# Opening of a four-layer graph kernel: x loaded whole, normalization and transposes two groups ahead

## What is computed

```python
h = relu(layernorm(x))
Wh = h @ W
e = leaky_relu(Wh @ a_src + (Wh @ a_dst).T)      # 0.2 below zero
h_attn = softmax(where(adj > 0, e, -9e15)) @ Wh
# dense branches from Wh: fe1/fe2, bcdt/abp, hz/out -> h_enh, hs
g = sigmoid(silu(ln([h_attn, hs] @ g1 + g1_b)) @ g2 + g2_b)
x = x + ln(g * h_attn + (1 - g) * hs + h_enh)
```

## Time and profile before

| what | us |
|---|---|
| three runs, median (lowest to highest) | 2624.14 (2617.22 to 2624.57) |
| profiled execution, its time | 2621.8 |
| its span, first to last instruction | 2620.1 |
| opening (first arithmetic of layer 0 starts) | 129.13 |
| mean granted TensorE clock | 0.95 |

### The profile page before, as it was taken

One profiled execution on the slowest core, in us unless ns is written; L12 is line 12 of the kernel. 1 busy time (PEld: TensorE's weight loads), 2 busy tenths in 40 slices (PEclk: granted clock), 3 DMA queues, 4 the chain that ended last, 5 costly groups with the idle time before them and its releaser, 6 DMA issues. The chain is left out here.

```text
span 2620.1 us, 45995 instructions
## 1 busy us (share of the span) xinstructions
PE 2309.3 (88%) x17238; PEld 1726.9 (66%) x17238; DVE 1836.5 (70%) x2939; ACT 1403.2 (54%) x2238; POOL 113.0 (4%) x124
## 2 busy tenths in 40 slices
PE   3489989889898896599995799999889999999998
PEld 2367767667676664488883577777635666666667
DVE  3396686777868764211115889898869889988896
ACT  3455545556454553466655545454436555655565
POOL 1000000100000000000000000000000000000000
PEclk8789999999999998799997899999989999999999
DMA  8343314224111100322221111112121111111110
GB/s 194 43 82 57 61 45 65 53 61 69 35 36 45 43 23 33 97 88 76 80 68 40 46 61 62 66 60 68 40 83 35 49 33 45 49 49 33 41 33 25
DMA packets 64523, 149.01 MB, mean 57 GB/s; under 512 B 10224, under 2 KB 15856, under 8 KB 63344
## 3 DMA queue, kind: packets, MB, share of 16 engines
q1 hardware_dynamic: 54560, 108.19, 13.3%
q0 software_dynamic: 5760, 33.56, 7.7%
q10 hardware_dynamic: 4048, 5.18, 0.6%
HBM read 172.05 MB, written 41.94 MB: 82 GB/s over the span
## 5 line engine op out<-in xcount | busy, mean ns | idle before, releaser
L1834 PE MATMUL bank<-VB,ph 128*128 128x257 f16 x2048 | 523.5, 281 | 97.0 <-DVE VB L1778 34.6
L1835 PE MATMUL bank<-VB,ph 128*128 128x257 f16 x2048 | 522.2, 280 | 0.0
L195 PE MATMUL bank<-s_row,kT_hi 128*128 128x512 f16 x1024 | 306.4, 381 | 6.8 <-DMA s_row<-qT_d 4.9
L1834 PEld LDWEIGHTS bank<-VB,ph 128*128 128x128 f16 x2048 | 204.1, 100 | 142.6 <-DVE pl L1773 55.8
L1353 PE MATMUL bank<-VA,ph 128*128 128x257 f16 x1024 | 281.9, 275 | 16.4 <-DVE pl L1025 10.9
L1838 PE MATMUL bank<-VB,pl 128*128 128x257 f16 x1024 | 292.0, 285 | 0.0
L2440 PE MATMUL bank<-VA,ph 128*128 128x257 f16 x1024 | 280.5, 274 | 3.0 <-ACT w_later_hi L2301 2.4
L1354 PE MATMUL bank<-VA,ph 128*128 128x257 f16 x1024 | 281.7, 275 | 0.0
L1355 PE MATMUL bank<-VA,pl 128*128 128x257 f16 x1024 | 281.6, 275 | 0.0
L2442 PE MATMUL bank<-VA,pl 128*128 128x257 f16 x1024 | 280.0, 273 | 0.0
L2441 PE MATMUL bank<-VA,ph 128*128 128x257 f16 x1024 | 280.0, 273 | 0.0
(11 more groups left out here) (322 smaller groups left out, 4760.9 us busy)
## 6 DMA issues: line engine op xcount, KB each, us to landing
mask<-mask_d SPq DMA_DIRECT2D x256, 256.0 KB, 2.8
mask_d<-in_adj POOLq DMA_DIRECT2D x8, 2048.0 KB, 23.4
xg<-in_x SPq DMA_DIRECT2D x16, 512.0 KB, 4.6
xg<-x SPq DMA_DIRECT2D x16, 512.0 KB, 4.2
x<-xo POOLq DMA_DIRECT2D x16, 512.0 KB, 2.9
w_d<-wr SPq DMA_DIRECT2D x8, 512.0 KB, 2.6
f<-w_d SPq DMA_DIRECT2D x8, 512.0 KB, 8.0
x<-xg SPq DMA_DIRECT2D x8, 512.0 KB, 3.9
```

The lines of the kernel that those rows point to most:

```text
L195: last = nc.tensor.matmul(out_ap, st, mv, start=(i == 0), stop=(i == len(todo) - 1))
L1834: nc.tensor.matmul(acc, p_hi, v_at(V, 0, t), start=first, stop=False)
L1835: last = nc.tensor.matmul(acc, p_hi, v_at(V, 1, t), start=False, stop=final and not weighted)
```

## The change

x is loaded whole, in five transfers on SP, ahead of the dense weights (moved from ACT's queue to SP's, fe1 first). wc moves to ACT's queue. Every statistic has a place of its own, so waits on reuse go. PE makes hT(1) ahead of Wh(0) and hT(g+2) behind Wh(g); ACT makes hT_hi(g+1), h(g+2), then keeps Wh(g); DVE takes moments three groups ahead. The bias rows lie as 18 partitions of 128, are split by DVE alone after group 1 and go by way of a DRAM tensor. The dense split is cut in four quarters (groups 2 to 5). The gate weights are loaded, in three 512 KB transfers, and split, in three pieces, in layer 0's first round, in buffers free until then. The first memsets of POOL are put in another order.

```diff
+                xg = sb(mem, "x_all", [P, G, R * D], F32)
+                brow = sb(mem, "brow", [NB, P], F32)          # NB = bias_n // P = 18
+                part = [sb(mem, f"part_{i}", [NB, P], F16) for i in range(3)]
...
@@ sync
-                    load_x(0)
-                    load(sp, wc[:, :, :], ...)
-                    load_x(1)
-                    load_x(2)
+                    for j, (g0, g1) in enumerate(((0, 1), (1, 2), (2, 4), (4, 6), (6, 8))):
+                        sp.dma_start(xg[:, g0:g1, :], ...).then_inc(s_x[j], 16)
+                    for dst, src in dense_in:
+                        load(sp, dst, src, s_w)
                     load(sp, bc[:, :], ...)
                     load(sp, kc[:, 0:1], ...)
+                    sp.wait_ge(zeroed.sem, zeroed.upto(2))
                     for dst, src in bias_rows:
-                        load(sp, dst, src.partition_broadcast(P), s_bias)
-                    load_x(3)
+                        load(sp, dst, src.rearrange("(k p) -> k p", p=P), s_bias)
                     for dst, src in column_in:
                         load(sp, dst, src, s_col)
-                    for g in range(4, G):
-                        load_x(g)
                     for i in range(3):
-                        sp.wait_ge(parted.sem, parted.upto(i))
-                        sp.dma_start(bias3[i:i + 1, 0:bias_n], part[i][i:i + 1, :]).then_inc(s_col, 16)
+                        sp.wait_ge(bias_cut.sem, bias_cut.upto(1 + 2 * i))
+                        sp.dma_start(bias_d[i:i + 1, :]..., part[i][:, :]).then_inc(s_part, 16)
+                    sp.wait_ge(s_part, 16 * 3)
+                    sp.wait_ge(zeroed.sem, zeroed.upto(5))
+                    sp.dma_start(bias3[0:3, 0:bias_n], bias_d[:, :]).then_inc(s_col, 16)
@@ scalar
+                    load(act, wc[:, :, :], ..., s_first)
-                    for dst, src in dense_in:
-                        load(act, dst, src, s_w)
-                    for dst, src in gate_in:
-                        load(act, dst, src, s_w)
                     make_h(0)
...
                     make_hT_hi(0)
+                    make_h(1)
                     for g in range(G):
                         if g + 1 < G:
-                            make_h(g + 1)
-                        if 1 <= g <= 3:
-                            bias_part(g - 1)
+                            make_hT_hi(g + 1)
+                        if g + 2 < G:
+                            make_h(g + 2)
                         keep_wh(g)
-                        if g + 1 < G:
-                            make_hT_hi(g + 1)
+                        if 2 <= g < 2 + pieces:
+                            if g == 2:
+                                act.wait_ge(s_w, 16 * len(dense_in))
+                            nc.scalar.copy(piece(w_dense[0], g - 2), piece(dense32, g - 2))
@@ vector
+                    def cut_bias():
+                        dve.wait_ge(s_bias, 16 * (2 + len(bias_rows)))
...
+                        nc.vector.tensor_tensor(brow[:, :], brow[:, :], arow[:, :], ALU.add)
+                        for i in range(3):
+                            nc.vector.tensor_copy(part[i][:, :], brow[:, :])
+                            if i < 2:
+                                nc.vector.tensor_tensor(brow[:, :], brow[:, :], part[i][:, :], ALU.subtract)
...
                     moments(0)
                     dve.wait_ge(s_first, 16 * 5)
...
+                    moments(1)
...
+                    shift_row(1)
                     make_hT_lo(0)
+                    moments(2)
                     for g in range(G):
                         if g + 2 < G:
-                            moments(g + 2)
+                            shift_row(g + 2)
                         if g + 1 < G:
                             make_hT_lo(g + 1)
+                        if g + 3 < G:
+                            moments(g + 3)
                         take_columns(g)
-                        if g + 2 < G:
-                            shift_row(g + 2)
+                        if 2 <= g < 2 + pieces:
+                            dve.wait_ge(weights_hi.sem, weights_hi.upto(g - 2))
+                            nc.vector.tensor_tensor(piece(w_dense[1], g - 2), piece(dense32, g - 2),
+                                                    piece(w_dense[0], g - 2), ALU.subtract)
+                        if g == 1:
+                            cut_bias()
@@ tensor
                     make_hT(0)
+                    make_hT(1)
                     pe.wait_ge(first_lo.sem, first_lo.upto(0))
                     for g in range(G):
-                        if g + 1 < G:
-                            make_hT(g + 1)
                         make_wh(g)
+                        if g + 2 < G:
+                            make_hT(g + 2)
@@ first_layer, sync, behind the first three masks and x of group 0
+                    for i, src in enumerate((g1_w[0:2 * P, :], g1_w[2 * P:4 * P, :], g2_w)):
+                        sp.dma_start(gate32[i]..., src...).then_inc(s_gate, 16)
@@ first_layer, scalar, end of pair hq of round i
+                            if i == 0 and hq in (4, 6, 8):
+                                if hq == 4:
+                                    act.wait_ge(s_gate, 16 * 3)
+                                nc.scalar.copy(gate_piece(0, hq // 2 - 2), gate32[hq // 2 - 2])
@@ first_layer, vector
+                            if i == 0 and hq in (5, 7, 9):
+                                dve.wait_ge(gate_hi.sem, gate_hi.upto(hq // 2 - 2))
+                                nc.vector.tensor_tensor(gate_piece(1, hq // 2 - 2), gate32[hq // 2 - 2],
+                                                        gate_piece(0, hq // 2 - 2), ALU.subtract)
```

More of the change, by code:

```diff
@@ L251, in build, with early_sem @@
         opened = []
+        def early_sem(name):
+            opened.append(early.enter_context(nc.semaphore(name)))
+            return opened[-1]
         def early_counts(*names):
-            made = [Count(early.enter_context(nc.semaphore(n))) for n in names]
-            opened.extend(made)
-            return made
+            return [Count(early_sem(n)) for n in names]
+        bias_d = nc.dram_tensor("bias_d", [3, bias_n], F16, kind="Internal").ap()
         s_mst = [sem(f"mask_stored_{i}") for i in range(3)]
         def opening():
-            XR = 3
+            NB = bias_n // P
             with ExitStack() as mem, nc.Block() as block:
@@ L268, in opening @@
                 dense32 = VA[:, 0:2 * sizes[0]].bitcast(F32)
-                gate32 = sb(mem, "gate32", [P, sizes[1]], F32)
-                xg = [sb(mem, f"xg_{i}", [P, R * D], F32) for i in range(XR)]
+                xg = sb(mem, "x_all", [P, G, R * D], F32)
                 h = [sb(mem, f"h_{i}", [P, R * D], F32) for i in range(2)]
                 hT = [[sb(mem, f"hT_{i}_{p}", [P, K, GW], F16) for p in ("hi", "lo")] for i in range(2)]
[L273 to L277, removed]
+                st = sb(mem, "st", [P, G * R, 6], F32)
+                mv = sb(mem, "mv", [P, G * R, 2], F32)
+                ve = sb(mem, "ve", [P, G * R], F32)
+                rstd = sb(mem, "rstd", [P, G * R], F32)
+                nb = sb(mem, "nb", [P, G * R], F32)
                 vecs = sb(mem, "vecs", [P, 2 * D], F32)
@@ L330, in opening, with piece @@
                     column_in.append((col_b[:, at:at + n], vec.rearrange("(k p) -> p k", p=P)))
+                pieces = 4
+                cut_at = [sizes[0] * i // pieces for i in range(pieces + 1)]
+                def piece(t, i):
+                    return t[:, cut_at[i]:cut_at[i + 1]]
                 @block.sync
                 def _(sp):
[L334 to L337, removed]
@@ L394, in make_h @@
                         for r in range(R):
-                            last = nc.scalar.activation(h[g % 2][:, r * D:(r + 1) * D], xg[g % XR][:, r * D:(r + 1) * D],
-                                                        ACT.Relu, bias=nb[g % 2][:, r:r + 1], scale=rstd[g % 2][:, r:r + 1])
+                            n = g * R + r
+                            last = nc.scalar.activation(h[g % 2][:, r * D:(r + 1) * D], xg[:, g, r * D:(r + 1) * D],
+                                                        ACT.Relu, bias=nb[:, n:n + 1], scale=rstd[:, n:n + 1])
                         last.then_inc(h_made.sem, 1)
@@ L447, in moments @@
                     def moments(g):
[L448 to L452, removed]
+                        dve.wait_ge(*x_here(g))
+                        for r in range(g * R, (g + 1) * R):
+                            last = nc.vector.bn_stats(st[:, r, :], xg[:, g, (r % R) * D:(r % R + 1) * D])
                         last.then_inc(moment.sem, 1)
                         dve.wait_ge(moment.sem, moment.upto(3 * g))
-                        if g:
-                            dve.wait_ge(shifted.sem, shifted.upto(g - 1))
-                        for r in range(R):
```

(38 more changed lines are left out.)

121 lines of the change are left out of this document (49 added, 72 removed).

## The result

| | before | after |
|---|---|---|
| median of the runs, us | 2623.84 (4 runs, 2617.22 to 2624.57) | 2579.27 (4 runs, 2575.95 to 2583.92) |
| profiled execution, its span | 2620.1 | 2582.2 |
| first arithmetic of layer 0 | 129.13 | 77.11 |
| from the first to the second whT_hi cast of layer 0 | 89.3 | 100.2 |
| mean granted TensorE clock | 0.950 | 0.954 |

The ratio is 0.9837, interval 0.9814 to 0.9860: 44.6 us less by the medians, 37.9 by the two profiled executions (the one of after is the slowest of its four). The forecast was 2584, range 2560 to 2602.

What follows compares the result with a forecast made beforehand. No engine was taken to bound the opening; later DVE, then PE from 2100 us. Layer 0's first masked tiles 42.5 us earlier, minus 3.4 gate split, plus 0.6 mask wait: 39.7 gained, median 2584, range 2560 to 2602.

Steps and rivals of the forecast that it cites:

- Head: Start of the opening: first weights land at 13 us (bounds 10.2 and 15), Wh(0) at 23.4 against 34.85 before.
- Groups: Opening's eight groups: reordering shortens the turn from 13.66 us to at most 6.0; 41.3 us in all, ending at 64.7.
- Layer 0 begins at 65: End of the opening: layer 0's first work comes at 65 us, 64 us earlier than before.
- the second copy's end (75): End of the opening: without free DMA between 45 and 53 us for SP's stores, layer 0 waits until 75.
- The starved masks: Layer 0's start: mask copies 1 and 2 back to back hold up mask loads until 96.5; 42.5 of 64 us stay.
- The gate loads, down before ACT wants them: Layer 0's first round: x and gate loads land by 102.6 us, before ACT needs them at tile 8, at 106.
- (c): Rival, opening's groups stay at 8 us, layer 0 at 85, gate loads meet copy 2: gain 36, 2586 us; chance 0.12.
- Gate split: Layer 0, tiles 10 to 19: three DVE subtractions add 3.4 us, all on the path; ACT's casts cost nothing.
- The sum: Whole kernel: 42.5 - 3.4 + 0.6 = 39.7 us gained, giving 2582, or 2584 for the median.
- (a): Rival, opening: copy 0 catches bias or dense loads, 13.4 us wait, layer 0 at 78.4, 2595 us; chance 0.27.
- (b): Rival, layer 0's masks: no crowding out by copies, a mask's 8 rows pass in one turn; gain 61, 2561; chance 0.13.
- (d): Rival, PE-bound stages: mean granted clock 2.3% lower costs 48 us, eating the gain and 8 more; chance 0.03.

Runs made afterwards that it cites:

- wc_on_sp: The changed kernel with the load of wc put back on SP's queue, behind x of group 0: 2591.1 us, ratio 0.9880 to the kernel before.
- chain_as_before: The changed kernel with only the order of the opening's loops put back (transposes of g+1 ahead of Wh(g)): 2611.2 us, ratio 0.9952 to the kernel before.

## Why the prediction was right, and where it was not

The queues of SP and ACT in the changed kernel, 8 to 10 us (answers to the earlier trace rows):

```profile
q1 hardware_dynamic: 97, 0.36, 57.5%
q10 hardware_dynamic: 95, 0.05, 15.2%
```

- **Head.** Forecast 13.0 for the first weights, measured 15.1, just above the upper bound given (15). I had taken ACT's queue at 83 packets a us after 4 us. It had 581 through by 8 us, where before it had 625, and 95 in 8 to 10 us instead of 166, 48 a us. So the two queues now went one for one. Why both were slower is open: SP's packets opposite are of some 4 KB before as well as after. That it is this load that sets the head is shown by wc_on_sp (folds at 11.28). From there to Wh(0) 10.2 us, forecast 10.4.
- **Groups.** 41.3 us forecast, 42.4 measured (25.3 to 67.7); the loop of 6.0 us measured 6.12, and the starts of Wh are 6.3, 4.2, 5.1, 6.1, 6.1, 6.1 and 4.2 us apart. The term is right, and chain_as_before shows that the order carries most of the gain.
- **Layer 0 begins at 65.** This step failed: it began at 77.1. I let a block end with its last work and SP's waits, and overlooked POOL's DRAIN, which was in the trace of before. The prediction has a start behind the second copy's end (75), but only for the case that this copy catches SP's stores, and it ruled that out; the stores were indeed done by 55.7. Of the 12.1 us missed, 9.4 are the DRAIN, the rest the late head and the groups.
- **The starved masks.** This step failed with it: copies 1 and 2 without a pause and masks starved until 96 cannot be while the block's end waits for copy 1. I had written that I am wrong if mask 0 lands within 5 us; it landed in 3.0. So by that sign the mechanism was wrong, and the 21.6 us charged for it were not lost: tiles 4 and 5 kept all of the 52.0 us.
- **The gate loads, down before ACT wants them.** Failed too: they were caught by copy 2. Rival (c) had this mechanism with its number, 31 us into the layer (measured 31.9), though for another reason for the late start.
- **Gate split** 3.4 forecast, 3.7 measured.
- **The sum.** Forecast: 64.1 us earlier, 21.6 lost to starved masks, 3.4 to the split. Measured at the second whT_hi, 41.2 us gained: 52.0 earlier, 7.2 lost to the gate loads, 3.7 to the split. Two errors near each other in size (12.1 us of DRAIN and late head not seen, 14.4 too much charged to starving) left the total close. The total was right though three of its steps were not, and that is luck: nothing ties the one error to the other. From the second cast on the lead wanders, 40.3 us at the end of layer 0, 41.7 at the start of the last layer, 37.9 at the end of the span; no run followed this, and it may be the spread between executions.
- **Rivals.** (a) did not occur, but was real: 4 us less on copy 0's time bring it out, with a wait of 13.15 us where it said 13.4, and 2592.6 where it said 2595; but layer 0 began at 89.8, not 78.4 (7.89 us of that are the DRAIN again), and the first masks were not starved, so that its total too comes near by errors that cancel. (b) is refuted by 32 packets against 32 and by a mask load issued at 85.1 that took 24.5 us. (c) was wrong in its conclusion: without the tighter order some 30 us are lost, not 2, for a turn is 10.7 to 12.2 us then, not the 8 I gave it, and copy 1 is issued with root(7), later too. (d) did not occur, the mean clock is 0.954.

In 36 to 40 us of the changed kernel 32 packets of SP's queue went against 32 of POOL's, over the 16 engines. The Trainium skill (DMA: Bandwidth & Descriptors, section Queues, rings and completion order) has this round robin by packet, and the trace agrees; its typical 9 to 17 descriptors in a packet no run here shows.

## What to carry to other kernels

Ask of every block's end which queues it waits for, transfers in flight on POOL's queue included: copy 1 was issued 33 us ahead of the block's end before, and its 24 us to landing cost nothing; 14 us ahead of the end of the other work its 23 us cost 9.4. And when a stage gets shorter, list the large copies that it used to cover, and what small loads are queued at the moment each starts: a copy that started 4.4 us sooner here cost 13 us.

## What the runs showed of the hardware that was not expected

The DRAIN at the end of POOL's part waits for its transfers to land: 23.8 us with a copy just issued, 6.4 with one that had been under way for 17 us, 1.2 with none, and in the first two it ends within 0.2 us of the landing. And a packet of 4 bytes waits for its turn beside a copy's packet of 16 KB as one of 2 KB does, so that column loads nearly stand still beside a copy: 32 packets in 4 us, against 1637 in 2 us alone.
